# A decoder layer on one Trainium2 core: the last two stages joined into one program per engine

## The reference

```
x = x + attention(layernorm(x))                      # 16 heads, position bias
x = x + cross(layernorm(x), ctx)                     # local attention without heads, then
        # a = layer_norm(attn + emb); layer_norm(relu(a @ w1 + b1) @ w2 + b2 + a)   "cross FFN"
x = x + ffn(layernorm(x))                            # "last FFN", quantised:
        # h = act_quant(x) @ weight_quant(w1).T; depthwise conv over tokens (3 taps); silu;
        # act_quant(h) @ weight_quant(w2).T
```

## Time and profile before

| | us |
|---|---|
| runs: lowest, median, highest | 3543.29, 3545.81, 3549.79 |
| the profiled execution's own time | 3542.34 |
| its span, first to last instruction | 3540.7 |
| what lies around the span | 1.64 |

### The profile page before, as it was taken

How to read it: one execution, slowest core, us unless ns; L and a number is a source line. 1 busy time by engine, 2 the same in 40 slices (tenths; PEclk the granted TensorE clock), 3 DMA queues, 4 the chain that set the end, 5 groups by cost and what they waited for, 6 DMA issues and landing times. The chain is left out here.

```text
span 3540.7 us, 57138 instructions
## 1 busy us (share of the span) xinstructions
PE 3167.0 (89%) x19234; PEld 2282.3 (64%) x19234; DVE 2344.0 (66%) x4197; ACT 1767.6 (50%) x3130; POOL 1171.8 (33%) x901
## 2 busy tenths in 40 slices
PE   6998999999999999789996998599999999368886
PEld 5776666666666666567775777487877788334443
DVE  5562788888888888644553888634445444379996
ACT  3331888888888888522323222132222222076662
POOL 2343311312231132144442455300111111058886
PEclk9999999999999999999998999799999999689999
DMA  6775311321222122355645443321111110201112
GB/s 216 239 243 169 85 60 56 92 62 56 73 79 61 56 85 68 122 181 188 228 171 184 129 131 118 108 84 42 42 42 43 42 42 29 82 22 55 60 42 72
DMA packets 239351, 350.53 MB, mean 99 GB/s; under 512 B 31792, under 2 KB 129104, under 8 KB 239184
## 3 DMA queue, kind: packets, MB, share of 16 engines
q1 hardware_dynamic: 208256, 290.41, 25.5%
q0 software_dynamic: 8912, 32.82, 2.8%
q10 hardware_dynamic: 22016, 25.17, 2.0%
HBM read 210.68 MB, written 137.64 MB: 98 GB/s over the span
## 5 line engine op out<-in xcount | busy, mean ns | idle before, releaser
L887 DVE CUSTOM_DVE_ANT_0 attend_scores<-attend_scores,attend_bias_table 128x1024 f32<-128x1024 f32 x512 | 630.5, 1232 | 164.8 <-PE attend_scores L741 161.5
L814 ACT ACTIVATE attend_probs<-attend_scores,attend_neg_max 128x1024 f32<-128x1024 f32 x512 | 571.7, 1117 | 141.0 <-DVE attend_neg_max L887 131.3
L753 PE MATMUL attend_turned<-ident,attend_probs 128*128 128x128 f32 x4096 | 557.3, 275 | 12.6 <-DVE attend_probsT L895 12.5
L753 PEld LDWEIGHTS attend_turned<-ident,attend_probs 128*128 128x128 f32 x4096 | 472.9, 141 | 121.4 <-DVE attend_probsT L895 30.2
L741 PE MATMUL attend_scores<-attend_k_stack,attend_q_stack 96*128 96x512 f32 x1024 | 373.4, 446 | 18.1 <-DMA attend_q_stack<-qk_parts 15.0
L822 ACT COPY attend_probsT<-attend_turned 128x512 f32<-128x512 f32 x640 | 359.5, 583 | 24.7 <-PE attend_turned L753 23.1
L2217 DVE TENSOR_TENSOR cross_ffn_h_lo<-cross_ffn_hidden,cross_ffn_h_hi 128x512 fp32r<-128x512 f32 x128 | 95.8, 753 | 363.7 <-ACT cross_ffn_h_hi L2114 363.1
L703 POOL TENSOR_TENSOR attend_out_parts<-attend_out_full,attend_out_parts 128x256 fp32r<-128x256 f32 x64 | 46.6, 727 | 847.3 <-ACT attend_out_parts L829 847.3
L768 PE MATMUL attend_out_acc<-attend_probsT,attend_v_in 128*32 128x256 f32 x4096 | 312.9, 389 | 0.7 <-DVE attend_out_full L905 0.7
L741 PEld LDWEIGHTS attend_scores<-attend_k_stack,attend_q_stack 96*128 96x128 f32 x1024 | 154.1, 190 | 175.2 <-issue 154.8
L895 DVE COPY attend_probsT<-attend_turned 128x512 f32<-128x512 f32 x384 | 263.5, 686 | 1.3 <-PE attend_turned L753 1.3
(11 more groups left out here) (294 smaller groups left out, 6644.5 us busy)
## 6 DMA issues: line engine op xcount, KB each, us to landing
qk_parts<-qkv_qk_out SPq DMA_DIRECT2D x64, 512.0 KB, 3.2
attend_k_stack<-qk_parts SPq DMA_DIRECT2D x192, 128.0 KB, 2.5
attend_q_stack<-qk_parts SPq DMA_DIRECT2D x192, 128.0 KB, 2.7
qkv_wq_raw<-L_ffn_w POOLq DMA_DIRECT2D x16, 1024.0 KB, 7.6
o_parts<-attend_out_parts ACTq DMA_DIRECT2D x64, 256.0 KB, 2.5
carried_o_in<-o_parts SPq DMA_DIRECT2D x32, 512.0 KB, 6.5
qkv_x_in<-x SPq DMA_DIRECT2D x8, 1024.0 KB, 5.7
v_rows<-qkv_v_out SPq DMA_DIRECT2D x32, 256.0 KB, 3.4
```

The lines of the kernel that those rows point to most:

```text
L753: last = pe.transpose(turned[:, x, c], probs[:, i % 2, k * P:(k + 1) * P], ident[:, :])
L814: act.activation(probs[:, i % 2], scores[:, i % 2], ACT.Exp, bias=neg_max[:, i % 4:i % 4 + 1], scale=-1.0, accum_out=den[:, qg % 2, j, h:h ...
L887: dve.tensor_tensor_reduce(scores[:, i % 2], scores[:, i % 2], bias_table[:, h, at:at + T], -1.0, BIG, ALU.add, ALU.min, neg_max[:, i % 4: ...
```

## The change

`both_ffns` takes the place of the two calls. `cross_ffn` and `quantised_ffn` no longer open a Block: each returns functions, one per engine, and one Block runs them one after the other. Both stages' semaphores live until the end, while the tiles are given back at the end of each function, so that the last FFN's tiles lie on the cross FFN's. The tiles are declared in another order, so that w1T, the x parts, the unit rows and w2T lie on w1_hi and w1_lo, and the PSUM tile `spread` on out_acc. Waits on the cross FFN's semaphores (`used`, `saved`) guard each reuse.

```diff
-def memory(nc, ctx, stage, own=True):
+def memory(nc, ctx, stage, own=True, tiles=None):
-        return ctx.enter_context(nc.sbuf_tensor(f"{stage}_{name}", shape, dt))
+        return (tiles or ctx).enter_context(nc.sbuf_tensor(f"{stage}_{name}", shape, dt))
...
 (cross_ffn, sync: the end)
             steps(sp, step)
+            next_loads(sp)
             store(NH - 1)
             store_x(NH - 1)
-                sp.wait_ge(stored, NH * 16)
-                for i in range(2):
-                    sp.wait_ge(xqT_stored[i], NH * HT // 2 * 16)
-                sp.wait_ge(unit_stored, NH * 16)
...
 (cross_ffn, tensor: the end)
             steps(pe, step)
+            next_products(pe)
             for t in range(HT):
                 turn_x(NH - 1, t)
...
+        used = dict(w1=(h_ready, NH * HB), w2=(out_ready, NH * HT), h_banks=(relu_done, NH * HB), out_banks=(out_read, NH * HT),
+                    turned_banks=(xqT_ready, NH * HT))
+        saved = dict(x2=(stored, 16), units=(unit_stored, 16), xq=[(xqT_stored[i], HT // 2 * 16) for i in range(2)])
...
 (quantised_ffn)
+        def load_x(sp, b):
+            past(sp, h_ready, 2 * (b - 1) * HB)
+            past(sp, edges_ready, b - 1)
+            for sem, count in saved["xq"]:
+                sp.wait_ge(sem, 2 * (b + 1) * count)
+            sp.dma_start(xqT[:, b % 2], xq_parts[b * TB:(b + 1) * TB].rearrange("t p n -> p t n")).then_inc(xq_loaded[b % 2], 16)
+            past(sp, y_ready, 2 * (b - 1) * HB)
+            past(sp, edges_done, b - 1)
+            sem, count = saved["units"]
+            sp.wait_ge(sem, 2 * (b + 1) * count)
+            sp.dma_start(unit_row[:, b % 2], row(x_units, b * T, T)).then_inc(unit_loaded[b % 2], 16)
+
+        def first_loads(sp):
+            sp.wait_ge(*used["w1"])
+            sp.dma_start(w1T[:, :, :], w1T_parts.rearrange("k p n -> p k n")).then_inc(w_loaded[0], 16)
+            load_x(sp, 0)
+            load_x(sp, 1)
+            sp.dma_start(w2T[:, :, :], w2T_parts.rearrange("f p n -> p f n")).then_inc(w_loaded[1], 16)
+
+        def sync(sp):
+            sem, count = saved["x2"]
+            sp.wait_ge(sem, UNITS * count)
+            for s in range(END):
...
+        def gpsimd(pool):
+            pool.wait_ge(*used["w1"])
             (loads of taps and conv_bias, memset of ones as before)
+            pool.wait_ge(*used["w2"])
             (memsets of y, waits and sem_inc as before)
...
+        def first_products(pe):
+            pe.wait_ge(*used["out_banks"])
+            pe.wait_ge(w_loaded[0], 16)
+            edge_products(pe, 0)
+
+        def tensor(pe):
+            pe.wait_ge(const_step, 6)
+            pe.wait_ge(*used["h_banks"])
+            pe.wait_ge(*used["turned_banks"])
...
+            pe.wait_ge(w_loaded[1], 16)
+            for s in range(END):
...
+        def scalar(act):
+            act.wait_ge(const_step, 6)
+            act.wait_ge(*used["out_banks"])
...
+def both_ffns(...):
+    with ExitStack() as ctx:
+        cross = cross_ffn(nc, ctx, ident, ...)
+        quantised = quantised_ffn(nc, ctx, ident, ..., cross["used"], cross["saved"])
         with nc.Block() as block:
             @block.sync
             def _(sp):
+                cross["sync"](sp, quantised["first_loads"])
+                quantised["sync"](sp)
             @block.gpsimd
             def _(pool):
+                cross["gpsimd"](pool)
+                quantised["gpsimd"](pool)
             @block.tensor
             def _(pe):
+                cross["tensor"](pe, quantised["first_products"])
+                quantised["tensor"](pe)
             (scalar and vector likewise)
...
-        cross_ffn(nc, ident, xw1, xb1, xw2, xb2, gamma, beta, a_rows, x1_rows, w_mean, x2_rows, xq_parts, x_units)
-        quantised_ffn(nc, ident, w1T_parts, conv_w, conv_b, w2T_parts, w_mean, x2_rows, xq_parts, x_units, rows(out))
+        both_ffns(nc, ident, xw1, xb1, xw2, xb2, gamma, beta, a_rows, x1_rows, w_mean, x2_rows, xq_parts, x_units,
+                  w1T_parts, conv_w, conv_b, w2T_parts, rows(out))
```

More of the change, by code:

```diff
@@ new lines, in edge_products @@
+        def edge_products(pe, b):
+            pe.wait_ge(xq_loaded[b % 2], (b // 2 + 1) * 16)
+            past(pe, scale_row_ready, 2 * b - 1)
+            for f in range(HB):
+                for k, col in ((0, P - 1), (1, 0)):
+                    for c in range(KB):
+                        last = pe.matmul(spread[:, 2 * f + k:2 * f + k + 1], w1T[:, c, f * P:(f + 1) * P],
+                                         xqT[:, b % 2, HT - 1 + k, c * P + col:c * P + col + 1], start=c == 0, stop=c == KB - 1)
+            last.then_inc(edges_ready, 1)
@@ L2406, in block_product @@
-                def block_product(i):
-                    u, f = divmod(i, HB)
-                    b, s = u // 2, u % 2
-                    past(pe, y_ready, i - ACC + 1)
-                    for c in range(KB):
-                        last = pe.matmul(acc[:, i % ACC], w1T[:, c, f * P:(f + 1) * P], xqT[:, b % 2, s * HT:(s + 1) * HT, c * P:(c + 1) * P],
-                                         start=c == 0, stop=c == KB - 1)
-                    last.then_inc(h_ready, 1)
-                def turn(i):
-                    u, f = divmod(i, HB)
-                    pe.wait_ge(silu_done, i + 1)
-                    past(pe, maxed, i)
-                    for t in range(HT):
-                        last = pe.transpose(turned[:, t], h[:, u % 2, f, t * P:(t + 1) * P], ident[:, :])
-                    last.then_inc(turned_ready, 1)
@@ L2460, in _ @@
-                for t in range(2):
-                    past(pe, out_done, (LAST - 1) * HT + t + 3)
-                pe.wait_ge(y_ready, SLOTS)
-                for f in range(HB):
-                    pe.wait_ge(hq_ready, LAST * HB + f + 1)
-                    for t in range(HT):
-                        last = pe.matmul(last_bank(t), hqT[:, LAST % 2, f, t * P:(t + 1) * P], w2T[:, f], start=f == 0, stop=f == HB - 1)
-                        if f == HB - 1:
-                            last.then_inc(out_ready, 1)
+                cross["tensor"](pe, quantised["first_products"])
@@ L2502, in _ @@
-                for s in range(END):
-                    if s < SLOTS:
-                        set_edge(s)
-                        taps_of(s)
-                    i = block_at(s, SILU_AT)
-                    if i is not None:
-                        silu(i)
-                    u = half_at(s, SPREAD_AT)
-                    if u is not None:
-                        act.wait_ge(spread_ready, u + 1)
-                        past(act, h_scaled_ready, (u - 1) * HB)
-                        act.copy(scale_row[:, u % 2], spread[:, :]).then_inc(scale_row_ready, 1)
+                cross["scalar"](act)
@@ L2515, in _ @@
+                quantised["scalar"](act)
             @block.vector
             def _(dve):
[L2517 to L2524 removed]
@@ L2609, in _ @@
-                for t in range(HT):
-                    finish(LAST * HT + t)
+                cross["vector"](dve)
+                quantised["vector"](dve)
 def decoder_layer(nc, x, ctx_1024, attn_Wqkv, attn_bqkv, attn_Wout, attn_bout, wq, bq, wk, bk, wv, bv, wo, bo, pos_bias,
```

984 lines of the change are left out of this document (499 added, 485 removed).

## The result

The changed kernel takes **3496.31 us** (median of 4 runs, 3491.6 to 3501.6) beside 3544.94 for the kernel before (4 runs): a ratio of 0.9865, 95% interval 0.9852 to 0.9879. The profiled execution has a span of 3491.2 us, 49.5 less than before. Medians in this document leave out one execution of experiment 1, which took 4745.23 us at a mean granted clock of 0.614. So the seam has to be set apart from the rest first, by reading the same edges in both traces.

The account below looks back on a forecast made before the run. DVE with its chain of slots was taken to pace the last stage, which started late behind the seam. Seam -36.9 and end +0.9 gave -36.0 us: 3509.8 from the median 3545.81, rounded 3509.5, range 3501 to 3519.

Parts of the forecast that it names:

- the seam: Cross FFN to last stage: block 0 starts 36.89 us earlier, right after ACT's last copy; 9.24 us of it for stores landing.
- tiles and banks lie elsewhere: Last stage's DVE dequantise with moved tiles: taken as nothing, bound plus or minus 1.4 us over 128 slots.
- E: Rival at the last stage's start: gain of 40 to 44 us by a full-clock ramp and shorter first slot; chance 0.04.
- SP's queue: Seam: six early load issues take 12.2 us, leaving 8 us of slack before the x2 store; cost nothing.
- The loads: Seam: issued at 3029.95, taking 26.65 us as before, so w2T lands about 3056.6, 12 us before needed.
- PE's queue: Seam: edge products of 3.55 us, now before the four turns, end by 3050 ahead of the first turn; cost nothing.
- DVE under the DMA: Cross FFN's tail: 7 MB of loads beside DVE's work taken as costing nothing, bound 0 to 0.3 us.
- Rival B: Seam: loads land late, sharing engines with stores and with SP held; gain 21.4 us, time 3524.4; chance 0.06.
- C: Rival at the seam: some engine's first work still waits for the last stores; time 3545.6 us; chance 0.02.
- D: Rival in the last stage: moved tiles lengthen DVE's operations or waits in every slot; slower, 3554.6 us; chance 0.02.
- The clock: PE's clock ramp at the last stage's start kept the same: zero, bounds -2.6 to +2.6 us.
- The end: Kernel's end: one clearing and one meeting move there, one Block exit goes; +0.86 us, bounds 0.7 to 1.1.

Follow-up runs that it names:

- e1: Kernel before with both new tile orders of the cross FFN (SBUF and PSUM), nothing joined: 3531.39 us, ratio 0.997.
- e3: Kernel before with the new SBUF tile order alone (aT, hidden and h tiles ahead of the bias columns): 3531.86 us, one run.
- e5: Kernel before with b1_cols declared last, so later cross FFN tiles such as aT_hi and h_hi start 64 bytes lower: 3529.72 us, ratio 0.9965.
- e4: Changed kernel with its first loads put behind the last stores and the edge products behind the turns, join kept: 3530.03 us, ratio 0.9962.
- e12: Changed kernel with edge products behind the turns and loads between the last turned tile's store and the units' store: 3522.19 us, ratio 0.9934.
- e8: Changed kernel with 96 bytes of padding ahead of all stages' tiles: 3491.52 us, ratio 0.9859.
- e10: Kernel before with b1_cols late and 64 bytes of padding: aT_hi and h_hi at their old bytes, weights 64 bytes higher; 3526.34 us, one run.
- e9: Changed kernel with padding so that every tile of every stage starts at a multiple of 128 bytes: 3490.24 us, ratio 0.9843.

## Why the prediction was wrong, and where it was right

**The step that failed** is "Second, tiles and banks lie elsewhere ... I take nothing; as bound ... plus or minus 1.4 us". It looked only at the last stage's tiles and only at DVE's dequantise. The change also reorders the *cross FFN's* tiles, and PE's products there are 3072 with two operands each. e3 and e5 show that term as about 12 us of gain (12.2 in e1 with both orders): over eight times its bound. None of the rivals names it; E's extra gain was to come from the ramp. The trace before did hold a sign of it, in the two paces of `mix_in` shown above, 227 and 233 ns. And what could have been seen without that is that the operands of 3072 products of 232 ns, 713 us of PE, are moved, so that each per cent unknown in a product's pace is 7 us of range. With 12.2 us taken off the forecast of 3509.5 it is 3497.3, and 3496.3 was measured (that it closes so nearly is partly luck, since the stages ahead took 2.3 us less and the last stage 2.2 more). The bounds printed as gains of 31.7 to 39.8 come to 31.5 to 40.2 by the prediction's own terms, which changes nothing.

**The seam was right in size**: 36.9 us forecast, 36.7 measured (39.46 less 2.74). Block 0 starts 0.26 us after the copy's end where 0.05 was taken. **One piece of it was misread**: the 9.24 us stands in the prediction as a wait for the units' store, and experiment 4 was expected to have it by the join. The join alone gave 2.8 of the 10.3 us (e4), since the same store then held the loads in the queue. What takes it away is that the loads are ahead of the store (e12, 10.05 us). The sum survived because the change does both.

**SP's queue**: all six issues took 11.3 us (3014.84 to 3026.17), 12.2 were forecast; the x2 store is issued 8.7 us later, so nothing waited. **The loads**: 26.0 us from the first issue to w2T's landing, 26.65 forecast, though w1T landed after 10.4 instead of 14.1. **PE's queue**: edge products 3028.36 to 3031.92, 11.5 us ahead of the first turn. **DVE under the DMA**: its tail took 31.62 us against 31.68, nothing, as taken. Rival B (late loads) is refuted for this kernel; loads that came late are seen in e4, where what held them was the 2 KB store ahead of them. C and D did not happen; the dequantise keeps its 673, 677 and 695 ns (lowest, median, highest).

**The clock.** The forecast kept the ramp. In the first 2 us of block 0 both kernels are at 0.50; then after the wait of 3.89 us for the first silu the kernel after still shows 1.00 where the earlier trace rows have 0.50, and falls behind it instead:

```profile
3053.00:3055.00 2.00, 1.47 (x4) 0.58 (x5) 0.00 (x0) 0.37 (x2) 0.00 (x0) 0.50 0.34 67
3063.00:3065.00 2.00, 0.32 (x3) 0.32 (x4) 0.41 (x1) 1.99 (x4) 1.56 (x2) 1.00 0.00 0
...
3067.00:3069.00 2.00, 2.00 (x8) 0.91 (x6) 1.93 (x3) 1.20 (x2) 0.43 (x1) 0.54 0.00 0
```

Slot 7's dequantise starts 16.12 us after the first, 16.17 before: the ramp is even, inside the bounds of 2.6. Later the stage falls behind: counted from the first dequantise, the 43rd is 2.4 us later than before, the last 1.3, and the last output 2.2. The mean clock of the stage is 0.93 for the earlier trace rows's 0.96:

```profile
3090.00:3480.00 390.00, 310.88 (x1787) 157.84 (x1813) 345.71 (x551) 235.14 (x464) 316.27 (x243) 0.93 0.16 49
```

That the clock's dips, which fall elsewhere now, make the 2.2 us fits these rows, but no run takes it apart, and the change need not be the cause. From the first dequantise to the last output is 429.0 us before and 431.3 after; the second trace of the changed kernel has 429.9, e8 429.5, and e10, which is the kernel before with other places, 432.0. One program's executions differ by about as much. The Trainium skill, TensorE: Matmul & The Clock Gate, "What's actually happening", would have the clock low when block 0 starts behind an idle array, and that is what both traces show; with the edge products moved away from block 0 the ramp got no longer.

**The end**: 0.3 us longer (4.20 to 4.52 from the last output to the last instruction), 0.86 forecast, 0.7 the lower bound: too small to matter, and outside its bounds.

The Trainium skill bears on the failed step as well. Its page SBUF — State Buffer, "A bandwidth-pool intuition that's wrong (but worth ruling out)", gives PE an independent second read port for the weights, from which one would expect that the places of the two operands don't matter to each other. Here they do: 232 ns for 227 between starts, by a shift of 64 bytes of either (e5, e10). By that rule the term is the zero that was taken, and the measured 12 us decide.

## What to carry to other kernels

When a change reorders or resizes tiles, it also changes where the operands of every product lie: before costing it at nothing, compare the starts of the stationary operand (the one loaded as weights) and the moving one modulo 256 bytes, and in a stage that PE bounds try the alignment as a change of its own, since it needs one padding tile or another order. When loads are freed from a wait for a store, ask whether that store still stands ahead of them in the same queue; here a store of small elements held them as long as the wait had. And to judge a seam, read the same edges in both traces, so that a gain from elsewhere isn't credited to it.

## What the runs showed of the hardware that was not expected

- Float32 products of 128x512 start every 227 ns when the tiles of the two operands start alike modulo 256 bytes and every 232 to 234 when they don't (cross FFN 232.4 to 227.0, projections 234 to 227, `mix_in` 233 to 227); alike modulo 128 was not enough. Slow were differences of 32 bytes (`mix_in`, `mix_out`), 64 (cross FFN), 96 (projections, 192 and 32) and 128 (both in e9); smaller ones don't occur here. In `mix_out` alignment gave less, 232.8 to 230, and why is open. So is what in the chip does it.
- A store of 512 elements of 4 bytes (2 KB, 8.7 to 10 us to landing) slowed 7 MB of loads issued behind it by some 10 us (e4 beside e12); the DMA engines moved under 100 GB/s for the first 15 us or so. With it behind the loads, it took 19 us itself and nobody waited.
- Issuing is not free either: SP was held 12.8 us by the issue of one x part behind that store (e4), and 0.57 to 9.20 by a unit row's (two of them in each trace).
